# A fused gated-attention block on one Trainium2 core: the routed FFN in two groups of batches instead of three, PSUM banks named by hand, and a new order of the work

## What is computed

```python
x = x + tanh(g_xattn[0]) * L0_xattn(layernorm(x), ctx)   # A: attention in both directions, gated mix
x = x + tanh(g_ffn[0])   * L0_ffn(layernorm(x))          # B: 8 experts of 256x256, the best one per token
x = x + tanh(g_xattn[1]) * L1_xattn(layernorm(x), ctx)   # C: 16 heads of 16, rotary embedding, softmax, output product
x = x + tanh(g_ffn[1])   * L1_ffn(layernorm(x))          # D: 8 experts 256->128->256 with gelu, top 2 of 8
```

```python
logits = x @ router_w.T + router_b; probs = softmax(logits)
y = (x @ expert_w[argmax(probs)].T + expert_b[argmax(probs)]) * max(probs)
```

## Time and profile before

| | us |
|---|---|
| median of three runs | 567.3 |
| lowest and highest | 567.3, 567.62 |
| the profiled execution's own time | 565.59 |
| span in its profile | 564.3 |
| PE busy, weight loads busy | 490.1 (87%), 424.1 (75%) |
| DVE, ACT, POOL busy | 347.4 (62%), 340.6 (60%), 281.0 (50%) |
| mean granted PE clock | 0.932 of full speed |

### The profile page before, as it was taken

How to read it: one execution, slowest core, us unless ns; L and a number is a source line. 1 busy time by engine, 2 the same in 40 slices (tenths; PEclk the granted TensorE clock), 3 DMA queues, 4 the chain that set the end, 5 groups by cost and what they waited for, 6 DMA issues and landing times.

```text
span 564.3 us, 11161 instructions
## 1 busy us (share of the span) xinstructions
PE 490.1 (87%) x3916; PEld 424.1 (75%) x3916; DVE 347.4 (62%) x848; ACT 340.6 (60%) x696; POOL 281.0 (50%) x363
## 2 busy tenths in 40 slices
PE   3888987999988998747877669999999999999997
PEld 2788987989987987735646448788797888777696
DVE  2466588465574756756364574785858577684455
ACT  2386574875855675212552476868878586658752
POOL 2054336635462654686171674757737384214154
PEclk9799988999999999656999777999999999899999
DMA  6412603235536456489577315124130312200001
GB/s 186 154 48 79 222 2 115 92 113 178 157 99 212 131 188 193 163 254 253 159 230 210 94 45 150 35 97 113 47 107 1 121 34 79 93 2 23 20 1 38
DMA packets 39595, 63.98 MB, mean 113 GB/s; under 512 B 6258, under 2 KB 19828, under 8 KB 39540
## 3 DMA queue, kind: packets, MB, share of 16 engines
q1 hardware_dynamic: 38004, 59.08, 34.1%
q0 software_dynamic: 1536, 4.20, 2.4%
HBM read 33.76 MB, written 12.45 MB: 82 GB/s over the span
## 4 chain that ended last, share of the span: by engine, by line
PE 49%; DVE 11%; issue 10%; ACT 9%; POOL 8%; SPq 6%; DMA 5%; another core or an unknown queue 1%; POOLq 0%; DVEq 0%; ACTq 0%
PE psum L354 10%; PE psum L356 9%; PE psum L355 9%; PE psum L578 3%; PE psum L511 3%; DMA xs<-slots_d 3%; SPq L2938 3%; PE psum L566 3%; PE psum L361 3%; ACT PT L1325 3%; PE psum L547 2%; DVE mpad L2128 1%; PE psum L401 1%; DVE xall L2070 1%; PE psum L587 1%
## 5 line engine op out<-in xcount | busy, mean ns | idle before, releaser
L2128 DVE TENSOR_REDUCE mpad<-psum 128x4 f32<-128x1024 f32 x64 | 77.8, 1220 | 31.9 <-PE psum L547 21.5
L1325 ACT ACTIVATE PT<-psum 128x1024 f32<-128x1024 f32 x64 | 65.5, 1023 | 23.3 <-PE psum L566 16.6
L2657 POOL TENSOR_TENSOR wA<-stage,wA 128x512 fp32r<-128x512 f32 x32 | 41.2, 1288 | 69.8 <-ACT wA L1372 67.4
L2197 DVE SCALAR_TENSOR_TENSOR xall<-psum,gat,xall 128x256 f32<-128x256 f32 x112 | 47.0, 477 | 12.6 <-PE psum L356 12.1
L2603 POOL TENSOR_SCALAR nm<-mv 128x2 f32<-128x2 f32 x32 | 7.7, 240 | 77.4 <-DVE mv L1912 70.2
L547 PE MATMUL psum<-st 48*128 48x256 f32 x256 | 33.0, 343 | 9.5 <-DVE mpad L2128 6.9
L511 PE MATMUL psum<-wt,xsT 128*128 128x256 f32 x148 | 38.9, 400 | 1.2 <-ACT xsT L1293 1.2
L354 PE MATMUL psum<-wB,wA 128*128 128x256 f32 x128 | 39.4, 308 | 0.6 <-DVE xall L2197 0.6
L566 PE MATMUL psum<-st 50*128 50x256 f32 x256 | 32.0, 330 | 8.9 <-ACT PT L1325 7.7
L1361 ACT ACTIVATE stage<-psum 128x512 f32<-128x512 f32 x32 | 19.1, 597 | 33.3 <-PE psum L356 33.0
L578 PE MATMUL psum<-PT,vv 128*32 128x256 f32 x512 | 36.7, 407 | 1.8 <-ACT PT L1325 1.8
(11 more groups left out here) (266 smaller groups left out, 1736.5 us busy)
## 6 DMA issues: line engine op xcount, KB each, us to landing
wt<-exp_d SPq DMA_DIRECT2D x37, 384.0 KB, 3.9
st<-parts SPq DMA_DIRECT2D x96, 128.0 KB
stage<-mats_d SPq DMA_DIRECT2D x21, 256.0 KB, 3.4
xs<-slots_d SPq DMA_DIRECT2D x37, 128.0 KB, 3.9
y_d<-ys SPq DMA_DIRECT2D x37, 128.0 KB, 3.5
cx<-ctx_d SPq DMA_DIRECT2D x16, 256.0 KB, 3.6
qr<-qp SPq DMA_DIRECT2D x32, 128.0 KB
slots_d<-ys SPq DMA_DIRECT2D x2, 1664.0 KB, 9.7
```

Source lines behind the costliest of these rows:

```text
L1325: e.activation(PT[:, i:i + 2, :, :].rearrange("p a k n -> p (a k n)"), ps2("ST", b, j).rearrange("p a n -> p (a n)"), ACT.Exp, scale=0.25) ...
L2128: e.tensor_reduce(mpad[:, :, 0:16].rearrange("p t (o a) -> p t o a", a=8)[:, :, :, j], ps2("max", b, j).rearrange("p o (t n) -> p t o n", ...
L2197: e.scalar_tensor_tensor(out=xall[:, b, t, :], in0=ps("dn", b, x)[:, t * 256:(t + 1) * 256], scalar=gat[:, b % 2, t, x:x + 1], in1=xall[:, ...
L2657: e.tensor_tensor(hlo[:, i, :], stage[:, n % 4, :], hh[:, i, :].bitcast(F32), ALU.subtract).then_inc(h_lo, 1)
```

## The change

- `GROUPS = [4, 4]`: two groups of 8 + 7 = 15 tiles, 30 tiles instead of 37. `rank(0)` and `rank(1)` follow the routing of batches 3 and 7. A group can now fill more than 8 tiles with one expert's tokens, so the comparison in `alloc` runs against 16 limits instead of 8 (`LIMS`, `over`). The two slot buffers are 15 tiles long instead of 13.
- Every PSUM bank is named at the call: `take(at, ...)` takes the bank given, `take2(at, ...)` the pair `at` and `at + 1`. The fixed rings are gone. In C and D, the maxima and exponentials use the pairs 4-5 and 6-7, the rest banks 0 to 3.
- The query bias products move out of `fold` into `fold_g`, with semaphores `t_gb` and `v_gb` of their own; PE calls `fold_g(i)` behind `fold(i)`.
- Some semaphores are merged (`v_hbg` into `v_htg`, `v_st0` and `v_st1` into `v_st`), and `ln_rstd` of B and D waits for its own preceding call.
- All five lists have a new order. `st0_init` (two memsets) is now the first call of DVE. On PE two batches of projections stand ahead of the first `P_T`; no tile is worked on before `gate(5)`; tiles 0 to 14 stand between `gate(5)` and `gate(7)`, tiles 15 to 29 among `c_max` of batches 0 and 1, and all `c_exp` stand behind tile 29. `c_qk(0)` and `c_v(0)` are behind `rank(1)`.

```diff
-GROUPS = [2, 3, 3]
+GROUPS = [4, 4]
+LIMS = 2 * max(GROUPS)
+TABW = LIMS + E * E + MAXT
...
-            def take(ring, *key):
-                banks = RINGS[ring]
-                k = banks[turn.get(ring, 0) % len(banks)]
-                turn[ring] = turn.get(ring, 0) + 1
-                if k in held:
-                    w.wait_ge(*emptied(*held[k]))
-                held[k], bank[key] = key, k
-                return psum[:, k, :]
+            def take(at, *key):
+                if at in held:
+                    w.wait_ge(*emptied(*held[at]))
+                held[at], bank[key] = key, at
+                return psum[:, at, :]
+
+            def take2(at, *key):
+                for k in (at, at + 1):
+                    if k in held:
+                        w.wait_ge(*emptied(*held[k]))
+                    held[k] = key
+                bank[key] = at
+                return ps2(*key)
...
+            def fold_g(i, at):
+                s, c = FUSED[i]
+                g = take(at, "gb", i)
+                w.wait_ge(v_cen, 5 * i + 5)
+                w.wait_ge(d_vec, 16)
+                for m in range(2):
+                    for k in range(2):
+                        last = e.matmul(g[:, m:m + 1], staged(c)[:, k * 256 + m * 128:k * 256 + m * 128 + 128], vec[:, VEC[s] + k:VEC[s] + k + 1],
+                                        start=(k == 0), stop=(k == 1))
+                last.then_inc(t_gb, 1)
...
+                else:
+                    w.wait_ge(p_rstd[name], 4 * b)
```

More of the change, by code:

```diff
@@ L696, in tensor_program @@
+            rank(0, 2)
+            proj("vc", 5, 0)
+            ln_T("A", 6, 1)
+            gate(4, 3)
+            proj("t0", 6, 2)
+            proj("t1", 6, 4)
+            P_T(0, 5, 5)
+            P_T(1, 5, 3)
+            proj("vs", 6, 6)
+            mix(4, 1)
+            PV(0, 5, 5)
+            PV(1, 5, 0)
+            scores(0, 6, 2)
+            proj("vc", 6, 0)
+            gate(5, 3)
+            moe_T(0, 0)
+            moe_T(1, 1)
+            moe_w(0)
             moe_w(1)
+            moe_T(2, 0)
@@ new lines, in tensor_program @@
+            c_exp(2, 1, 4)
+            c_max(4, 2, 6)
+            c_PV(0, 1, 0)
+            c_exp(3, 1, 4)
+            c_exp(4, 1, 6)
+            c_max(5, 2, 4)
+            c_PV(1, 1)
+            c_exp(5, 1, 6)
+            c_exp(6, 1, 4)
+            c_PV(2, 1, 1)
+            c_max(6, 2, 6)
+            c_exp(7, 1, 4)
+            c_qk(4, 2, 3)
+            c_max(7, 2, 4)
+            c_PV(3, 1)
+            ln_T("D", 0, 2)
+            c_v(4, 0)
+            c_maxT(2, 1)
+            d_up(0, 0, 3)
@@ new lines, in tensor_program @@
+            d_up(1, 1, 3)
+            c_maxT(3, 0)
+            route_D(1, 1)
+            c_qk(5, 3, 0)
+            c_max(0, 4, 4)
+            c_max(1, 4, 6)
+            c_v(5, 1)
+            c_out(2, 2, 0)
+            c_exp(0, 3, 4)
+            c_exp(1, 3, 6)
+            d_down(7, 0, 3)
+            d_down(0, 1, 0)
+            d_down(1, 1, 2)
+            d_up(2, 1, 3)
+            c_max(2, 4, 4)
+            c_max(3, 4, 6)
+            c_PV(0, 3, 0)
+            ln_T("C", 6, 1)
+            c_outT(2, 2)
@@ new lines, in tensor_program @@
+            ln_T("D", 2, 0)
+            c_maxT(4, 2)
+            c_PV(2, 3, 3)
+            c_v(6, 2)
+            c_PV(3, 3)
+            route_D(2, 0)
+            c_out(3, 1, 2)
+            d_up(0, 2, 3)
+            c_outT(3, 1)
+            d_up(1, 2, 2)
+            c_max(0, 5, 4)
+            c_max(1, 5, 6)
+            d_up(2, 2, 0)
+            d_up(3, 2, 3)
+            c_max(2, 5, 4)
+            c_max(3, 5, 6)
+            c_wo(3, 0)
+            d_down(6, 1, 1)
+            c_exp(0, 4, 4)
@@ new lines, in tensor_program @@
+            c_exp(1, 4, 6)
+            d_down(7, 1, 0)
+            d_down(0, 2, 2)
+            d_down(1, 2, 3)
+            c_max(4, 5, 4)
+            c_max(5, 5, 6)
+            d_down(2, 2, 0)
+            d_down(3, 2, 1)
+            c_PV(0, 4, 2)
+            c_exp(2, 4, 4)
+            c_exp(3, 4, 6)
+            c_qk(7, 1, 0)
+            c_exp(4, 4, 4)
+            c_exp(5, 4, 6)
+            c_PV(1, 4)
+            ln_T("D", 3, 1)
+            d_down(4, 2, 0)
+            d_down(5, 2, 3)
@@ new lines, in tensor_program @@
+            d_down(7, 2, 1)
+            c_exp(0, 5, 4)
+            c_exp(1, 5, 6)
+            c_v(7, 0)
+            c_max(3, 6, 4)
+            c_max(4, 6, 6)
+            d_down(0, 3, 2)
+            c_PV(0, 5, 0)
+            c_exp(2, 5, 4)
+            d_down(1, 3, 1)
+            d_down(2, 3, 3)
+            c_max(5, 6, 4)
+            c_exp(3, 5, 6)
+            d_down(3, 3, 1)
+            ln_T("D", 4, 2)
+            d_down(4, 3, 3)
+            c_exp(4, 5, 4)
+            c_exp(5, 5, 6)
```

2312 lines of the change are left out of this document (1070 added, 1242 removed).

## The result

The changed kernel takes 541.98 us (median of four runs, 540.63 to 543.69) where the kernel before took 567.3 (560.48 to 567.62); the ratio is 0.962, with a 95% interval of 0.957 to 0.968. The forecast had 559.6 and a range from 547 to 573: the direction was right, the size was not, and the time lies outside the range. The profiled execution took 540.63 us, 1.3 above its span of 539.3.

The account below looks back on a forecast made before the run. PE was taken to bound the kernel from 104 to 229.8 us and after 360, not between. Stretches of 219.9, 21.5, 56 and 259.2 sum to a 556.6 us span; with 3.0 above span, 559.6 us, range 547 to 573.

Parts of the forecast that it names:

- to the last rank: Start to the last rank: 173.5 us counted work plus 41.4 loss, corrected by -4, +4 and +5, gives 219.9.
- the memsets (-4): In alloc(0)'s wait before: st0's two memsets, now first on VectorE, take 4 us off; 0 if not covered.
- the chain behind gate(7) (+4): gate(7) to rank: less PE work to cover the chain, and gathers ahead of ln_rstd B(7), add 4 us; between 0 and 9.
- dense tiles (+5): First group: 15 tiles share 41 us of counted work, 2.7 each, nothing to spare; adds 5 us, between 0 and 14.
- Rank to first tile: Last rank to the second group's first tile: 18.9 us before, two more scatters of 1.27 us, so 21.5 us.
- The second group: Its 15 tiles take 56 us, last product at 297.4; lower bound 41 us, upper bound DMA, 67 or 51 us.
- the exposed second group: Rival, slower: DMA keeps 223 GB/s, last product at 305.0, stall before D's second batch stays 18 us; 574 us; chance 0.23.
- The 51 us: Second group's DMA time for 15.0 MB at 296 GB/s, the best 5 us, counted from the first load's issue.
- After the last product: Last product to end: 231.2 us counted work plus 28 loss (11 until D's second ln_T, then 17), 259.2 us.
- Named banks change no instruction: Whole kernel, banks of C and D included: naming the banks costs nothing, so no time was taken for it.
- the order itself gains: Rival, ahead of tile 0: new order fills PE's waits, half of the other 20 us lost saved; 549.6 us; chance 0.20.
- The front gives it back: Rival, no change: first group's tiles at 3.5 us, all gathers reach the chain, rank at 228; 567.7 us; chance 0.14.

Follow-up runs that it names:

- The two cuts: The kernel before and the changed kernel, each cut down to stage A on all engines, x after A stored as output: 198.06 us and 169.88 us.
- all four such moves in the old stage A: Old cut with projections ahead of P_T 228.41 us, gate and mix later 210.5, mix further 205.34; full kernel before with gate one piece later 586.88.

## Why the prediction was wrong

**The step that failed is the first of the sum, "to the last rank": 219.9 forecast, 198.2 measured, 21.7 early.** Its work term stands (173.5 counted). The loss term doesn't: I carried 41.4 us over from the kernel before and corrected it only for the memsets (-4), the chain behind gate(7) (+4) and dense tiles (+5), as if the loss belonged to stage A and not to its order. No reason stood there for carrying it over. The trace had shown that only 7.3 of the 28 us ahead of tile 0 were waiting for weights; I made the rest a rival at 0.20 and half its size. The range's low end, 547, even left out that rival at its full 20 us (539.6). Measured, the loss there went from 28 to 11 us by the same count, of the 20 us in question 16.5 were saved. The two cuts show that stage A's new lists do this without any change of groups. Of the corrections, the memsets show no effect (tried in both kernels); the chain from gate(7) to rank(1) took 17.3 us (180.89 to 198.16), where 15 and 2 for the gathers were forecast, so that the +4 stands; the fifteen tiles came from 138.1 to 181.3, 3.1 us each with 2.7 us of waits for xs and its copy in all, so they had room, and the +5 was nothing.

**Rank to first tile: 21.5 forecast, 29.7 measured.** I added two scatters and stopped there. What I had not read is the order of SP's and POOL's lists at this place. `load_tile(15)` stands third: its xs is issued at 219.84, 3.0 us behind that of tile 16, where before tile 24's was first and its transposes came 2.3 us behind its issue:

```profile
246.35 0.69 SPq L2898 DMA_DIRECT2D xs<-slots_d  x1
```

On PE tile 15 stands behind c_qk(1), which waits 10.4 us for a product that POOL makes behind eight scatters; and PE runs the rest of it at half clock (0.50 from 220 to 225). In this trace PE's list is what decides: the xs loads there landed at most 2.9 us behind their issue, so tile 15's was there by 222.8, 3 us later than forecast, and PE came 5 us after it. Moving the context's part took 3.3 us off in one trace and 1.0 in another, since the next wait stands close behind. So the missing 8 us are the way over PE's list, with the wait for ln_T C(2) and the way over the loads (3 us too long by itself) close behind it; they are not a sum of the two.

**The second group: 56 forecast, 56 measured** (227.83 to 284.0), at a DMA share of 0.76, 216 GB/s. That it fits is in part luck. The tiles began 8 us late, but their loads had not: tile 16's were issued at 213.35 and 216.80.

```profile
216.80:284.00 67.20, 47.61 (x252) 38.00 (x254) 25.34 (x40) 17.41 (x46) 31.04 (x32) 0.79 0.75 212
```

The rival of the exposed second group counted from the first load: 67.3 us for 15.0 MB. From the first xs load it is 67.2 us, and from the first wt load 70.65 us at 211 GB/s, which is 14.9 MB. So its bytes and, nearly, its rate held; what it had wrong is that the first load goes 3.7 us ahead of the first tile, which was 11 to 14.5 here. Put behind the measured rank, it has the last product at 283.3, the forecast at 275.7, and the trace at 284.0. The close fit is chance (from first xs load to last output it was 67.0 us here and 61.8 to 65.0 in three further traces), and whether DMA or PE's list sets this stretch was not tried.

One reading behind these bounds was wrong. The earlier trace rows is the best 5 us of the last group's stage, not of the trace, which has

```profile
55.00:60.00 5.00, 4.59 (x40) 4.58 (x40) 1.89 (x3) 4.19 (x10) 1.28 (x3) 1.00 1.04 364
```

where the zeroes for the slots are written. So the sentence that the trace does not show the quoted rate, with 296 GB/s as its best stretch, is wrong: 364 lies above it for 5 us. The 51 us stand for the last group's stage alone, and DMA is not free while the zeroes are written (a share of 1.04).

**After the last product: 259.2 forecast, 255.3 measured.** The split was wrong: to D's first batch 13.6 us were lost where before 6.3 had been, and then only 10.5 where 28.4 had been. Of these 17.9 us, idle PE is 5.6 (14.6 to 9.1), and 4.0 of it are waits of c_exp and c_max for their banks' readers. Before, from 320.8 on:

```profile
PE psum L566 <- ACT PT L1325: 3.7, 6, 1.1
PE psum L547 <- DVE mpad L2128: 0.5, 2, 0.3
```

and after, from 325.45 on:

```profile
PE psum L555 <- ACT PT L1318: 0.2, 1, 0.2
```

The larger part, 12.3 us, is PE busy beyond the counted work, and 6.3 of it lie between D's first two batches, where the clock was 0.79 before and 1.00 after. Before:

```profile
320.80:360.35 39.55, 34.72 (x271) 27.10 (x272) 24.74 (x53) 28.48 (x48) 26.11 (x27) 0.79 0.31 88
```

The cause of the other 6 us (clock 0.99 before, 1.00 after) stays open.

"Named banks change no instruction" was true and missed the point. Nor was it right that stalls by a bank don't stand out: over the whole trace before, c_exp waits 7.7 us for PT and c_max 6.9 for mpad, which are among the largest of PE's waits, and such waits fall from 14.6 to 6.6 us. That the new order doesn't bear the fixed pairs of the kernel before is shown by the 70 us; how much of the end's gain is the banks' and how much the order's is open, since the new order was not run with rings.

Of the rivals, "the order itself gains" was the right one; its 10 us are 0.6 of what was saved. With 16.7 at that place it would have said 542.9, but that this is so near is luck: the measured path was also 5 us shorter up to the rank, 8.2 longer behind it and 3.9 shorter at the end. "The front gives it back" did not happen; of "the exposed second group" the time from the first load came true and the longer end did not.

Two theories of mine about the mechanism fell behind the prediction. It is not one cover, and not two: each batch has three chains that leave PE and come back, and the context's low parts besides. Shown is that the new lists together leave fewer waits (PE idle 25.4 for 42.8 us in the cuts), the largest part of the difference, 6.7 us, at P. That they work by serving all chains at once is an argument, and which move carries how many of the 28 us can't be said, since they don't add up: POOL's order alone takes 20 back and gate's place alone 64.

## What to carry to other kernels

When a change brings a new order, the idle time of the old one is not a constant to be carried over: split it by releaser, set aside what no order can fill (here 7.3 us for the first load), and give the rest a term of its own with both ends in the range. For each chain that leaves the bounding engine and returns, compare its length with the work that stands in between, before and after, in all of the lists and not in one. And a piece moved by hand into a fixed order can uncover one chain as it covers another: all four such moves in the old stage A cost time, 7 to 30 us by the medians.

## What the runs showed of the hardware

Idle time on PE mostly cost more than its length, but not by a fixed price. The seven cuts of stage A run the same 1128 matmuls:

| cut of stage A | idle us | busy us | mean granted clock |
|---|---|---|---|
| after | 25.4 | 143.0 | 0.967 |
| after, POOL in the old order | 38.3 | 151.1 | 0.938 |
| before | 42.8 | 154.0 | 0.945 |
| before, gate a batch later, mix further | 47.3 | 159.4 | 0.929 |
| before, gate and mix a batch later | 55.0 | 152.9 | 0.957 |
| before, projections ahead of P_T | 65.1 | 159.4 | 0.907 |
| after, gate behind PV | 68.7 | 165.5 | 0.877 |

Idle is the span less PE busy. From the first row to the last 43.3 us of idle time bring 22.5 us of longer work, about half of their own length on top, and the mean granted clock is 0.877 for 0.967; in the whole kernel with fixed pairs the clock is 0.885 and PE is busy 506.1 us where the changed kernel has 472.3. But the rows don't stand in one line: the fifth has 12.2 us more idle time than the third and is busy 1.1 us less, at a higher clock. Against the first row a microsecond of idle time went with 1.3 to 1.8 us of span in the other rows (28.4 for 17.4 in the third); between two of the later rows it can be 0.9. So a forecast that adds up waits alone came out short here against the new order, and no single factor mends it.
